# A gated mixture behind a recurrent mixer on one core: the head in a new order, and the rows of the last projection laid down tile by tile

## What is computed

```
xn  = (x - mean) / sqrt(var + eps)
xm  = xn * time_mix + previous(xn) * (1 - time_mix)
k   = exp(min(xm @ Wk.T, 60)); v = xm @ Wv.T; r = xm @ Wr.T
wkv, sum_k = sum over earlier u of Wm[t,u] * (k*v)[u], Wm[t,u] * k[u]   (+1e-16)
s   = (sigmoid(r) * wkv / sum_k) @ Wo.T
e   = argmax(xn @ Wg + bg)                  # one of 8 experts for each token
g   = silu(relu(xn @ W1[e] + b1[e]) @ W2[e] + b2[e])
out = x + s * g
```

## Time and profile before

| | |
|---|---|
| three runs | 176.46, 176.85, 175.15 us; median 176.46 |
| profiled execution | 175.93 us; span from first to last instruction 174.1 us, so 1.83 us lie around it |
| mean granted clock of TensorE | 0.963 of full speed |
| busy share of the span | PE 86%, PE weight loads 68%, DVE 71%, ACT 59%, POOL 57% |
| chain that ended last | PE 66%, issue 7%, ACT 6%, DMA 5%, POOL 4%, DVE 4% |

### The profile page before, as it was taken

One profiled execution on the slowest core, in us unless ns is written; L12 is line 12 of the kernel. 1 busy time (PEld: TensorE's weight loads), 2 busy tenths in 40 slices (PEclk: granted clock), 3 DMA queues, 4 the chain that ended last, 5 costly groups with the idle time before them and its releaser, 6 DMA issues.

```text
span 174.1 us, 3350 instructions
## 1 busy us (share of the span) xinstructions
PE 149.5 (86%) x954; PEld 119.0 (68%) x954; DVE 122.8 (71%) x262; ACT 102.4 (59%) x295; POOL 98.5 (57%) x149
## 2 busy tenths in 40 slices
PE   7995899996797689995999794985999999999960
PEld 2433465442575477874789693885999999999960
DVE  2498994999999999999999999999600000000971
ACT  2946975976484366564782922744886677642720
POOL 7879920017777475764455876746564464460550
PEclk9999999999699969999699999999999999999997
DMA  4943999706354142342323631543645552115973
GB/s 80 318 155 136 386 295 341 292 3 210 106 166 124 34 161 90 109 168 85 111 86 116 211 105 49 171 147 105 230 153 178 175 178 96 45 45 184 361 297 120
DMA packets 15808, 27.96 MB, mean 161 GB/s; under 512 B 2952, under 2 KB 3520, under 8 KB 15792
## 3 DMA queue, kind: packets, MB, share of 16 engines
q1 hardware_dynamic: 12944, 23.10, 37.7%
q0 software_dynamic: 2272, 4.66, 9.5%
q10 hardware_dynamic: 576, 0.01, 0.2%
HBM read 10.78 MB, written 6.75 MB: 101 GB/s over the span
## 4 chain that ended last, share of the span: by engine, by line
PE 66%; issue 7%; ACT 6%; DMA 5%; POOL 4%; DVE 4%; another core or an unknown queue 3%; ACTq 2%; DVEq 0%
PE ps L1064 21%; PE ps L1047 20%; PE ps L1079 9%; PE ps L989 7%; DMA wg<-in_L_ffn_Wg 3%; PE ps L948 3%; DMA xg<-xn_rows,gidx 2%; PE ps L1038 2%; PE ps L939 2%; PE ps L1059 1%; ACT ohhi_hidif L857 1%; POOL ser L441 1%; DVE ohlo L607 1%; ACT kT L875 1%
## 5 line engine op out<-in xcount | busy, mean ns | idle before, releaser
L467 POOL DMA_INDIRECT g_rows<-gout,sidx x39 | 40.1, 1028 | 25.4 <-ACT gout L866 18.6
L460 POOL DMA_INDIRECT xg<-xn_rows,gidx x32 | 34.0, 1064 | 33.3 <-DVE gidx L658 15.8
L1047 PE MATMUL ps<-xn_sb,w1e 128*128 x312 | 43.7, 282 | 3.8 <-issue 3.7
L1047 PEld LDWEIGHTS ps<-xn_sb,w1e 128*128 128x128 f32 x312 | 39.9, 198 | 4.6 <-issue 4.6
L857 ACT ACTIVATE ohhi_hidif<-ps,b1T 128x128 f32<-128x128 f32 x104 | 30.2, 384 | 19.1 <-PE ps L1047 16.9
L1064 PE MATMUL ps<-w,ohhi_hidif 128*128 x208 | 29.6, 282 | 2.5 <-issue 2.5
L748 DVE TENSOR_TENSOR kT<-ps,kT 128x512 f32<-128x512 f32 x8 | 5.3, 688 | 37.3 <-ACT kT L917 36.4
L989 PE MATMUL ps<-xmT,wT 128*128 128x512 f32 x48 | 25.7, 649 | 4.5 <-ACT rT L877 1.9
L1064 PEld LDWEIGHTS ps<-w,ohhi_hidif 128*128 128x128 f32 x208 | 25.6, 192 | 5.6 <-issue 5.3
L866 ACT COPY gout<-ps 128x128 f32<-128x128 f32 x39 | 11.1, 284 | 15.7 <-remote 10.1
L857 ACT ACTIVATE hidT<-ps,b1T 128x128 f32<-128x128 f32 x52 | 15.0, 380 | 8.3 <-remote 4.2
(11 more groups left out here) (165 smaller groups left out, 220.1 us busy)
## 6 DMA issues: line engine op xcount, KB each, us to landing
w1e<-w SPq DMA_DIRECT2D x39, 256.0 KB
x_sb<-in_L_attn_x SPq DMA_DIRECT2D x8, 256.0 KB, 6.1
w<-in_L_ffn_W SPq DMA_DIRECT2D x1, 2048.0 KB, 9.5
xn_rows<-xn_sb SPq DMA_DIRECT2D x2, 1024.0 KB, 12.4
kT<-g_rows SPq DMA_DIRECT2D x8, 256.0 KB, 4.4
out_x<-kT SPq DMA_DIRECT2D x8, 256.0 KB, 2.1
g_rows<-gout,sidx POOLq DMA_INDIRECT x39
xg<-xn_rows,gidx POOLq DMA_INDIRECT x32
```

Of the source, the lines that this page charges most:

```text
L460: g.indirect_dma_start(xg[j][:, :], None, xn_rows, bass.IndirectOffsetOnAxis(gidx[:, s:s + 1], 0)).then_inc(gathered[j], 16)
L467: g.indirect_dma_start(g_rows, bass.IndirectOffsetOnAxis(sidx[:, s:s + 1], 0), gout[j][:, :], None).then_inc(scattered[j], 16)
L1047: last = t.matmul(psH[n % DEEP][:, cols], w1e[n % W1_RING][:, cols], xgT[:, bass.ds(held.of(n), 1), :].rearrange("p o t -> p (o t)"), star ...
```

## The change

Six things are changed at once.

1. The 32 normalisations are shared anew. POOL: 8 tiles of the first half, 4 of the second. DVE: 2 and 8. ACT: 6 and 4. POOL does them ahead of its decay series, and takes over from DVE the splitting of b2 into three bf16 parts.
2. ACT's order in the head: `deviation(1)` stands before `copy_xnT(0)`, the copy of `wT` behind that, and its tiles of the second half between the copies of blocks 1 to 3. PE turns the weights first of all.
3. Two kvr more stand ahead of the inversion on PE (`INV_AFTER` is 10, and the ACT table change stays behind the eighth).
4. PE loads its registers before it turns the first gathered rows, and waits for W2 only at the third slot. SP issues W2 behind the two stores of normalised rows.
5. `attend` writes `rw[q]` tile by tile: the 512 results in four runs of 128, and `project` takes each run as a contiguous stationary operand. DVE's two large writes then have a step of 128 elements.
6. The addresses of `b1T` and `w2` are formed from a register and a constant: the operation ahead of each matmul of layer 2 has three register steps instead of four.

```diff
@@ -48,17 +48,25 @@
 K_CLAMP = 60.0
-INV_AFTER = 2 * NBB
+TANH_AFTER = 2 * NBB
+INV_AFTER = TANH_AFTER + 2
 EARLY = 3 * NBB
...
 TAYLOR = 9
+POOL_TILES = [(0, 1)] * NBB + [(0,)] * NBB
+DVE_TILES = [(3,)] * 2 + [()] * 2 + [(1, 3)] * NBB
+ACT_TILES = [(2,)] * 2 + [(2, 3)] * 2 + [(2,)] * NBB
 SMALL_DECAY = 0.5
...
 BK = 3 * BQ
+def tiles_upto(tiles, k):
+    return sum(len(tiles[m]) for m in range(k + 1))
@@ -128,6 +136,7 @@
         w2 = sb("w2", [P, E * HC, P])
+        w2_e = w2[:, :, :].rearrange("p (e c) d -> p e (c d)", c=HC)
         wnat = sb("wnat", [P, 4, P])
@@ -141,6 +150,7 @@
         b1T = sb("b1T", [P, BQ])
+        b1T_e = b1T[:, :].rearrange("p (e c) -> p e c", c=HC)
         tmix = sb("tmix", [P, 1])
@@ -342,15 +352,16 @@
             sp.dma_start(w1[:, :, :], W1.rearrange("e d h -> d e h")).then_inc(ld_w1, 16)
-            sp.dma_start(w2[:, :, :], W2.rearrange("e (c p) d -> p (e c) d", p=P)).then_inc(ld_w2, 16)
...
             for b in range(BATCH):
...
                 sp.dma_start(xn_v[:, b * NBB:(b + 1) * NBB, :, :],
...
                              ).then_inc(xn_stored, 16)
+            sp.dma_start(w2[:, :, :], W2.rearrange("e (c p) d -> p (e c) d", p=P)).then_inc(ld_w2, 16)
@@ -431,6 +442,14 @@
+            for k in range(NB):
+                if k % NBB == 0:
+                    pool.wait_ge(ln_ready, k // NBB + 1)
+                for j in POOL_TILES[k]:
+                    n = k * TPB + j
+                    g.tensor_scalar(xn_sb[:, n, :], x_sb[:, n, :], rstd[:, n:n + 1], nbias[:, n:n + 1],
+                                    ALU.mult, ALU.add).then_inc(xn_pool, 1)
             pool.wait_ge(dec_ready, 1)
@@ -443,15 +462,18 @@
-            for k in range(NB):
-                if k % NBB == 0:
-                    pool.wait_ge(ln_ready, k // NBB + 1)
-                for j in range(2):
-                    n = k * TPB + j
-                    last = g.tensor_scalar(xn_sb[:, n, :], x_sb[:, n, :], rstd[:, n:n + 1], nbias[:, n:n + 1],
-                                           ALU.mult, ALU.add)
-                last.then_inc(xn_pool, 1)
+            pool.wait_ge(ld_bias, 16 * 4)
+            step.link(g.tensor_copy(b2_part[:, 0, :], b2_nat[:, :]))
+            step.link(g.tensor_tensor(b2_rest[:, 0, :], b2_nat[:, :], b2_part[:, 0, :], ALU.subtract))
+            step.link(g.tensor_copy(b2_part[:, 1, :], b2_rest[:, 0, :]))
+            step.link(g.tensor_tensor(b2_rest[:, 1, :], b2_rest[:, 0, :], b2_part[:, 1, :], ALU.subtract))
+            step.link(g.tensor_copy(b2_part[:, 2, :], b2_rest[:, 1, :]))
+            for j in range(3):
+                rows = slice(j * BQ, (j + 1) * BQ)
+                last = g.tensor_copy(b2_rows[rows, :], b2_part[rows, j, :])
+            last.then_inc(bias_ready, 1)
+            pool.wait_ge(bias_ready, 1)
             def gather(s):
@@ -525,17 +547,14 @@
-            own_tiles = [n for n in range(NT) if n % TPB == 3]
+            own_tiles = [k * TPB + j for k in range(NB) for j in DVE_TILES[k]]
+            in_first = tiles_upto(DVE_TILES, NBB - 1)
...
                                 ALU.mult, ALU.add).then_inc(xn_dve, 1)
-            def normalise_first_half():
-                if normalised[0] < len(own_tiles) // 2:
-                    normalise_tile()
@@ -555,12 +574,12 @@
             finish_stats(0, go_on=stats_tile)
-            for _ in range(len(own_tiles) // 4):
+            for _ in range(in_first):
                 normalise_tile()
...
             step.link(last)
-            finish_stats(1, go_on=normalise_first_half)
+            finish_stats(1, go_on=lambda: None)
             while normalised[0] < len(own_tiles):
@@ -607,23 +626,9 @@
-            def split_bias():
...
             dve.wait_ge(omt_ready, 1)
...
             mix_shifted(1)
-            split_bias()
             pick_experts(0)
@@ -686,7 +691,7 @@
                 n0 = step.n
...
                 if q % NBB == 0:
@@ -720,15 +725,19 @@
                 dve.wait_ge(dve_step, n0 + SIGNUM)
-                v.scalar_tensor_tensor(out=rw[q][:, half_a], in0=num[:, 0:BLK // 2 - 1], scalar=0.5,
-                                       in1=rden[:, half_a], op0=ALU.mult, op1=ALU.mult)
+                by_tile = rw[q].rearrange("p (j r) -> p r j", j=TPB)
+                in_time = lambda t, s: t[:, s].rearrange("p (r j) -> p r j", j=TPB)
+                lower, upper = slice(0, BLK // 2), slice(BLK // 2, BLK)
+                v.scalar_tensor_tensor(out=by_tile[:, 0:P // 2, :], in0=in_time(psG[:, :], lower), scalar=0.5,
+                                       in1=in_time(rden, lower), op0=ALU.mult, op1=ALU.mult).then_inc(dve_step, 1)
+                dve.wait_ge(dve_step, n0 + RDEN_B)
+                v.scalar_tensor_tensor(out=by_tile[:, P // 2:P, :], in0=in_time(psG[:, :], upper), scalar=0.5,
+                                       in1=in_time(rden, upper), op0=ALU.mult, op1=ALU.mult)
+                dve.wait_ge(dve_step, n0 + RW_A)
                 v.scalar_tensor_tensor(out=rw[q][:, 0:1], in0=sig0[:, :], scalar=0.5,
-                                       in1=rden[:, 0:1], op0=ALU.mult, op1=ALU.mult)
-                dve.wait_ge(dve_step, n0 + RDEN_B)
-                v.scalar_tensor_tensor(out=rw[q][:, half_b], in0=num[:, BLK // 2 - 1:BLK - 1], scalar=0.5,
-                                       in1=rden[:, half_b], op0=ALU.mult, op1=ALU.mult).then_inc(rw_ready, 1)
+                                       in1=rden[:, 0:1], op0=ALU.mult, op1=ALU.mult).then_inc(rw_ready, 1)
                 dve.wait_ge(rw_ready, q + 1)
-                step.n = n0 + RDEN_B
+                step.n = n0 + RW_A
@@ -781,10 +790,11 @@
-                n = k * TPB + 2
                 act.wait_ge(ln_ready, k // NBB + 1)
-                s.activation(xn_sb[:, n, :], x_sb[:, n, :], ACT.Identity, bias=nbias[:, n:n + 1],
-                             scale=rstd[:, n:n + 1]).then_inc(xn_act, 1)
+                for j in ACT_TILES[k]:
+                    n = k * TPB + j
+                    s.activation(xn_sb[:, n, :], x_sb[:, n, :], ACT.Identity, bias=nbias[:, n:n + 1],
+                                 scale=rstd[:, n:n + 1]).then_inc(xn_act, 1)
@@ -809,28 +819,30 @@
                 normalise(k)
+            deviation(1)
             copy_xnT(0)
-            deviation(1)
+            act.wait_ge(wT_ps, 1)
+            s.copy(wT[:, :, :].rearrange("p t d -> p (t d)"), psW[:, :]).then_inc(wT_ready, 1)
             copy_xnT(1)
+            normalise(4)
+            normalise(5)
+            copy_xnT(2)
+            normalise(6)
+            normalise(7)
+            copy_xnT(3)
             act.wait_ge(ld_small, 16 * 2)
             mix_here(0)
-            copy_xnT(2)
-            mix_here(1)
-            copy_xnT(3)
-            for k in range(NBB, NB):
-                normalise(k)
             act.wait_ge(ld_bg, 16 * TPB)
...
             copy_xnT(4)
+            mix_here(1)
+            copy_xnT(5)
             mix_here(2)
-            copy_xnT(5)
             copy_xnT(6)
...
             copy_xnT(7)
+            copy_logits(1)
             mix_here(4)
-            copy_logits(1)
-            act.wait_ge(wT_ps, 1)
-            s.copy(wT[:, :, :].rearrange("p t d -> p (t d)"), psW[:, :]).then_inc(wT_ready, 1)
             act.wait_ge(b1T_ps, 1)
@@ -855,7 +867,7 @@
                     last = s.activation(hidT[n % DEEP][:, cols], psH[n % DEEP][:, cols], ACT.Relu,
-                                        bias=b1T[:, bass.ds(experts.of(n) * HC + c, 1)])
+                                        bias=b1T_e[:, bass.ds(experts.of(n), 1), c:c + 1].rearrange("p o c -> p (o c)"))
                 last.then_inc(hid_ready, 1)
@@ -876,12 +888,12 @@
-            for m in range(INV_AFTER):
+            for m in range(TANH_AFTER):
                 copy_kvr(m)
...
             s.activation(sqrt_eps[:, :], eps[:, :], ACT.Exp)
-            for m in range(INV_AFTER, EARLY):
+            for m in range(TANH_AFTER, EARLY):
                 if m == EARLY - 1:
@@ -930,9 +942,9 @@
...
                 if k >= 2:
@@ -989,6 +1001,10 @@
+            pe.wait_ge(ld_proj, 16 * 4)
+            for m in range(4):
+                last = t.transpose(psW[:, m * P:(m + 1) * P], wnat[:, m, :], ident[:, :])
+            last.then_inc(wT_ps, 1)
             transposes(0)
@@ -1006,10 +1022,6 @@
             logits(7)
-            pe.wait_ge(ld_proj, 16 * 4)
-            for m in range(4):
-                last = t.transpose(psW[:, m * P:(m + 1) * P], wnat[:, m, :], ident[:, :])
-            last.then_inc(wT_ps, 1)
             logits_by_token(1)
@@ -1062,7 +1074,7 @@
                     last = t.matmul(Y_BANK[n][:, 0:P], hidT[n % DEEP][:, cols],
-                                    w2[:, bass.ds(e * HC + c, 1), :].rearrange("p o d -> p (o d)"),
+                                    w2_e[:, bass.ds(e, 1), cols].rearrange("p o d -> p (o d)"),
                                     start=False, stop=c == HC - 1)
@@ -1076,7 +1088,7 @@
```

(10 more changed lines are left out.)

24 lines of the change are left out of this document (7 added, 17 removed).

## The result

The changed kernel took 182.33, 181.52 and 180.61 us, the kernel before 176.46, 176.85, 175.15 and 175.25: ratio 1.039, 95% interval 1.031 to 1.048. It is **slower**, and the forecast of 176.0 us with its range of 172.5 to 178.6 was wrong.

The account below looks back on a forecast made before the run. The chain was taken as mostly PE, with gain only from an earlier slot start or shorter tail: 175.93 + 0.5 (later slots) - 1.0 (tail) = 175.4, a median of about 176.0 us, range 172.5 to 178.6.

Parts of the forecast that it names:

- The split of b2 and the series, on POOL: POOL before the first gather: 10 us at most of work fits in 15.78 us of idle time, so no cost.
- The last sentence of the prediction: Slots: the forecast would be wrong if a pause of ACT or PE that no semaphore explains came or went; unpriced.
- Head, +0.45: Normalisation to logits: ACT's list makes the fourth copy of xnT start at 19.65 against 18.96, costing 0.45 us.
- Two kvr, gidx +1.8: PE's inversion: seven kvr ahead start it near 38.5, so gidx comes at 39.95 instead of 38.15, 1.8 us later.
- Registers ahead: PE before the slots: loads during the gathers take 2.8 us off the path; second tile turned at 44.9 to 45.2.
- The half clock: Start of the slots: a sign, the clock at half for about 3.5 us after the second gathered tile is turned.
- W2, addresses, nothing: W2's load behind the stores, and one register step less in layer 2: both hidden, no gain or loss.
- rw by tile: Projection and tail: 64 passes take 7.6 us instead of 14.95, DVE's wait goes, -1.0 us; DVE's writes become 0.9.
- The slower rival: POOL's queue: gathers late for good, pauses at slots 1 and 2, clock low; 179.0 us, 177.3 without the clock; chance 0.17.

Follow-up runs that it names:

- a_nob2: Changed kernel with the splitting of b2 back on DVE, nothing else undone; 1.011 to the kernel before, on a chip with pauses.
- a_again: Changed kernel once more, unchanged, on a chip with pauses; 1.029 to the kernel before.
- a_nob2_inv8: Changed kernel with b2's splitting back on DVE and the two kvr behind the inversion again; 0.997 to the kernel before, on a chip with pauses.
- a_inv8_2: Changed kernel with the two kvr behind the inversion again, on a chip with pauses; 1.025 to the kernel before.
- b_b2: Kernel before plus rw's layout, PE's register loads ahead of the rows, and b2's splitting on POOL; medians 180.92 / 177.49 = 1.019, no interval.
- a_addr: Changed kernel with the old address forms of b1T and w2; 1.0049 to the kernel before, on the chip without pauses.
- a_inv8: Changed kernel with the two kvr behind the inversion again; 1.0002 to the kernel before, on the chip without pauses.
- a_regs: Changed kernel with PE's register loads behind the first gathered rows again; 1.0242 to the kernel before, on the chip without pauses.
- b_rw_regs: Kernel before with rw's layout and PE's register loads ahead of the first gathered rows, nothing else; 1.000 to the kernel before, on a chip with pauses.
- b_rw: Kernel before with the layout of rw alone; 0.9955 to the kernel before, on the chip without pauses.

## Why the prediction was wrong

- **The step that failed** is the term put at nothing: "The split of b2 and the series, on POOL. [...] fit behind its last tile at about 20. Nothing." The cover was there: POOL was idle 11 us before its first gather. What the sum did not hold is that the first gather then starts 0.57 us later behind gidx, and that a chip with late announcements loses some 2% with the split on POOL: a_nob2 against a_again (1.011 against 1.029) and a_nob2_inv8 against a_inv8_2 (0.997 against 1.025, on two chips) show it, and b_b2 agrees. That the 0.57 us are the way from the one to the other is not shown. The two kvr cost another 0.4 to 1.4%. The 3.9% of the result are not added up in full: which chip it came from is not on record, and on another the change was at 1.029.
- **The sum took the slots for fixed** at before's 108.5 us ("The change touches no matmul of the slots. So it can gain only by [...]"). On this chip about 20 of these us are pauses and their after-effects, by the 88.6 of the other chip, and they depend on things that no semaphore of the kernel shows. The slots came to 113.9. The prediction read them as "PE nearly without a gap in their second half", but from 100 to 120 us PE was busy for 15.45 of 20. The last sentence of the prediction names such pauses as what would make it wrong, and gave them no price: before's trace had ACT waiting 3.4 to 3.8 us at three places (59.56, 80.93 and 95.67 us), one with "remote" as its releaser and two with layer 1. That was the warning to put into the range.
- **Head, +0.45:** measured 0.05 at the logits. The vectors came sooner than reckoned, by 0.36 us for the first half (ACT's first tile at 11.95 against 12.31) and 0.3 for the second (POOL's at 17.20 against 17.5), and the fourth copy of xnT ran at 19.18, not 19.65.
- **Two kvr, gidx +1.8:** +1.0. The inversion ran at 38.16 instead of 38.5 and its 32 matmuls in 0.95 instead of 1.3. On a quick chip the two kvr cost up to 0.8 us with the clock (a_addr against a_inv8, the addresses included), on those with pauses 0.4 and 1.4%.
- **Registers ahead:** the place is right, second tile at 45.12 in 44.9 to 45.2. That is in part luck: gidx came 0.8 us sooner than reckoned, and the first gather 0.57 us later behind it, so it was issued at 40.21 where the sum had 40.4. What the loads took off the path is 1.2 us by a_regs and b_rw_regs, not 2.8. The half clock came, but for 6.8 us and from 43.2, while PE waited for the first tile, not for 3.5 behind the second.
- **W2, addresses, nothing:** not refuted. W2's place is at 1.031 against 1.029. The old addresses never ran beside the changed kernel on one chip (1.019 against 1.025 is for unlike kernels).
- **rw by tile:** right. 0.114 us a pass against 0.119 forecast, the wait of DVE gone, and 0.7 us gained against 1.0 (b_rw), since silu comes next (0.74 <-ACT at 169.21). DVE's two large writes went from 0.36 and 0.42 us to 0.54 and 0.60, not 0.9. The Trainium skill (SBUF — State Buffer, Door 1: The DMA port swizzle), by which a new line of 16 bytes costs, agrees in direction on both sides.
- **The slower rival** forecast the direction by the wrong mechanism (gathers late for good). The third tile was turned at 48.92, 0.7 later than before, and PE did not wait for it: it came straight from kvr.

What stays open: why PE's ends are announced late on some chips, and how b2 on POOL makes more of it. The Trainium skill (Runtime: NRT & Kernel Launch, Instruction fetch mechanics) says that crossing to a new block of instructions is mostly hidden. The trace of b_rw agrees: eight transfers of 16 KB in the queue of instructions, which I take for PE's refills, fall into or ahead of its slots, and PE has no gap there. They took 0.9 to 1.5 us on both kinds of chip, so their duration doesn't tell the two apart. On the chips with pauses the long one at slot 3 begins within 1.5 us of the end of such a transfer in every trace that has it (55.44 and 55.55 us in the changed kernel), while later pauses stand far from one (6.0 us at 102.7). That PE lacked instructions there is a rival that no run tested. Whether the recording of the profile takes part was not tried.

## What to carry to other kernels

Before a sum is made, split each stage's time into work and pauses, and where the releaser is "remote" or no semaphore explains it, treat that stage's time as uncertain by the size of those pauses; here they and what follows them were 20 of 108 us, and more of them made the loss. An edit that is free by cover can still move when its engine's next DMA is issued: look at the gap between index and first gather before and after. And price a change on more than one chip: the change without its addresses stood at 1.005 on one and at 1.019 on another.

## What was not expected of the hardware

- The same program takes 157.3 us on one chip and 175.6 to 177.5 on three others and the one of the result. The head is as long on both kinds (inversion at 36.58 in b_rw, 36.45 in before) and so is the first gather (1.25 us).
- On the slower ones PE's ends are announced in bunches: the ends of successive groups, each of eight matmuls, come 0.09 to 0.10 us apart (61.01 and 61.10 in the changed kernel), where eight matmuls take about 1.1. Between two bunches up to 11 us pass (b_b2, 48.99 to 60.04).
- The first indirect DMA of POOL starts 0.87 instead of 0.31 us behind its index when small copies and subtractions, and the wait for them, preceded it, 11 us or more earlier; its duration is 1.36 to 1.39 against 1.25.
